# The routing-weight product of a two-block transformer kernel: contraction over 128 rows in place of a 32-row tile

## The chip, the core and the metric

The kernel runs on one core of a Trainium2 chip. The metric is device time in microseconds (us) from launch to end; the smaller the better. A core has five engines that work side by side and wait for each other through semaphores: TensorE (PE, with the weight loads shown apart as PEld), VectorE (DVE), ScalarE (ACT), GpSimd (POOL) and SyncE (SP), which starts the transfers here. TensorE multiplies a stationary operand, loaded first, with a moving operand that streams past it, and writes to one of eight PSUM banks; the other engines work in SBUF and read PSUM (POOL has no use of PSUM here).

## The reference

Two blocks run one after the other, each with attention and a feed-forward part, on 1024 tokens of width 256. Only the last part, a mixture of 16 experts of which each token uses 6, matters here:

```
logits = xf @ gate_w.T
probs = softmax(logits)
routing_weights, selected = top_k(probs, 6)
combine = zeros((T, 16)).at[arange(T)[:, None], selected].add(routing_weights)
act = silu(xf @ w1_gate.T) * (xf @ w1_up.T)          # 16 experts x 176 hidden columns
moe_out = einsum('te,tei,ehi->th', combine, act, w2)
out = x + moe_out + shared_out
```

`combine[t, e]` multiplies all 176 hidden columns of expert `e` for token `t`.

## The kernel before

**Numbers.** A product that must be exact to float32 is made of three fast products (`mm3`, L554): each operand is split into a high part, rounded to the type `float32r`, and the rest, and hi*hi, hi*lo and lo*hi are summed in PSUM.

**The last stage ("moe").** The hidden columns of the shared expert (3 chunks, j = 0 to 2) and of the 16 experts (22 chunks of 128, j = 3 to 24) stand one after the other; the tokens are in two halves of 512. A step (j, half) makes 12 products of 512 columns for gate and up. For j of 3 and more one product more follows on L690: it spreads the routing weights. Its stationary operand is a slice of 128 columns of `SELr`, a table of 32 rows that holds a one where a hidden column belongs to an expert (16 rows for the high part of the weights, 16 for the rest); its moving operand is 512 columns of `CTr`, the transposed routing weights of the half. The result is, for 128 hidden columns by 512 tokens, the weight that each must be multiplied with. There are 44 such products, 22 for each half. Then come 12 products of 256 columns (`down`) for the step before this one.

**Who feeds whom.** After a step ACT makes silu of the gate part (L1010), DVE multiplies it with the up part (L1357) and with the spread weights (L1364), ACT rounds it to its high part `VVh` (L1017), DVE subtracts to get the rest `VVl` (L1369), and TensorE's `down` takes both. One `down` is always a step behind, so that this chain has a whole step's time. PSUM banks 4 to 7 go round for gate, up and spread; banks 0 to 3 hold the sums.

**Order of the work.** A function `plan` writes one list of items, and each engine works through its own items in that order. Ahead of the moe steps stand `endnorm` (the last normalization; POOL's part is L1605), the splitting of the weight chunks moe3 and moe4 on POOL (L1654, L1656) and `selector` on POOL (L1694), which rounds `SELf`, as the transfer brought it, into `SELr`. `spread` turns the routing weights of a half on TensorE (L867) and ACT copies them into `CTr` (L1115). `latent_end()` names the events after which the memory of the attention stage may be overwritten.

Of the kernel before, what the change touches and what calls it, by code (L numbers as in the profile page):

```python
# [7 lines left out]
F32 = mybir.dt.float32  # L8
R32 = mybir.dt.float32r
BF16 = mybir.dt.bfloat16  # L10
I32 = mybir.dt.int32
ALU = mybir.AluOpType
# [3 lines left out]
T = 1024  # L16
# [35 lines left out]
class Signals:  # L52
# [10 lines left out]
    def mark(self, kind, *key, by=1):  # L63
        self.count[kind] = self.count.get(kind, 0) + by
        self.value[(kind,) + key] = self.sem(kind), self.count[kind]
        return self.sem(kind), by
# [4 lines left out]
    def at(self, kind, *key):  # L71
        return self.value.get((kind,) + key, (None, 0))
# [286 lines left out]
def build(nc, x, w, sm, sel, out):  # L359
    with ExitStack() as outer:  # L360
        S = Signals(lambda name: outer.enter_context(nc.semaphore(name)))
        B = Banks()
        program(nc, outer, S, B, x, w, sm, sel, out)


def program(nc, outer, S, B, x, w, sm, sel, out):
    mark, at, now = S.mark, S.at, S.now

    def sb(name, shape, dt=F32, ctx=outer):
        return ctx.enter_context(nc.sbuf_tensor(name, shape, dt))  # L370
# [89 lines left out]
    m1 = ExitStack()  # L460
# [1 line left out]
    U2 = [sb(f"U2{i}", [128, 512], ctx=m1) for i in range(3)]  # L462
    VV = [(sb(f"VVh{i}", [128, 512], R32, ctx=m1), sb(f"VVl{i}", [128, 512], R32, ctx=m1)) for i in range(3)]
    SELf = sb("SELf", [32, 22 * 128], ctx=m1)
    SELr = sb("SELr", [32, 22 * 128], R32, ctx=m1)
    CTr = sb("CTr", [32, T], R32, ctx=m1)
    parts += [(sb(f"yh{i}", [128, SLOT], R32, ctx=m1), sb(f"yl{i}", [128, SLOT], R32, ctx=m1)) for i in range(2)]
    m1.close()

# [8 lines left out]
    def bank(*key):  # L478
        return banks[B.of(*key)]
# [4 lines left out]
    def have(*key):  # L484
        return at(f"full{B.of(*key)}", *key)

    def vacates(*key):

        return S.sem(f"free{B.of(*key)}"), 1
# [10 lines left out]
    def half_cols(half):  # L500
        return slice(half * 512, half * 512 + 512)
# [35 lines left out]
    def latent_end():  # L537
        return have("lo", 3), at("hi", "u", n_units - 1), at("x3", 3), at("pn2", n_units - 1, 1)
# [364 lines left out]
    def scalar(x):  # L903
        e = Waits(x)
# [203 lines left out]
            x.activation(pr[:, hs, 0:16], pr[:, hs, 0:16], ACT.Exp).then_inc(*mark("ge", half))  # L1108

        def spread(half):  # L1110
            if half == 0:
                for s in latent_end():
                    e.wait_ge(*s)
            e.wait_ge(*have("sp", half))
            x.copy(CTr[:, half_cols(half)], bank("sp", half)[0:32, :]).then_inc(*vacates("sp", half))  # L1115

        run(order, {"norm1": norm1, "fuse": fuse, "turn1": turn1, "project": project, "headnorm": headnorm,
                    "turnqk": turnqk, "masks": masks_, "score": score, "pturn": pturn, "turnqm": turnqm, "turnat": turnat,
# [479 lines left out]
    def gpsimd(x):  # L1598
        e = Waits(x)
# [90 lines left out]
            rsqrt(rs, ve, half, "ve4", "rs4")  # L1690

        def selector():
            e.wait_ge(*at("sel"))
            x.tensor_scalar(SELr[:, :], SELf[:, :], 1.0, 0.0, ALU.mult, ALU.add).then_inc(*mark("selr"))  # L1694

        run(order, {"norm1": norm1, "rotate": rotate, "mask": mask, "l0begin": l0begin, "split": split, "memnorm": memnorm,
                    "memturn": memturn, "ffnmean": ffnmean, "expert": expert, "latstd": latstd, "l1norm": l1norm,
# [155 lines left out]
```

## Time and profile before

| what | value |
|---|---|
| median of 3 runs | 826.01 us (824.09 to 826.27) |
| the profiled execution | 827.4 us, of which 825.6 us are the span from the first to the last instruction |
| granted TensorE clock, mean | 0.946 of full speed |
| busy: PE / PEld / DVE / ACT / POOL | 741.5 / 599.1 / 473.3 / 322.4 / 245.0 us |
| chain of work that ended last, by engine | PE 71%, DVE 15%, ACT 5%, issue 5%, POOL 3% |
| the chain by line, first three | L554 48%, L649 4%, L620 4%; L690 2% |

All times in a trace count from the start of the span. A row of the timeline gives the start, the duration, the engine, the line and what is written and read; matmuls are pipelined, so that one starts before the one ahead of it has ended, and the distance from start to start, not the duration, says what one costs. "128\*128 128x512" is a tile of 128 rows by 128 columns of the array, and 512 columns of moving data; "32\*128 32x512" is a tile of 32 rows. The moe stage reaches from 567 us to the end.

### The profile page before, as it was taken

Reading aid. Unit: us, or ns where it says so; the run is one execution under the profiler, and the core shown is the slowest. Engines: PE = TensorE matmul, PEld = TensorE weight load, DVE = VectorE, ACT = ScalarE, POOL = GpSimd, SP = SyncE. Lnnn points to the kernel's source line nnn. Section 1 sums busy time; section 2 is a strip of 40 time slices with the busy share of each in tenths; the row PEclk is TensorE's granted clock in tenths of the full one; section 3 lists DMA queues with packets and bytes.
Section 4 is the critical chain, followed back from the end, with each engine's and each line's share of the span. In section 5 each row is a group of like instructions: output and inputs, shape, how many; then the busy total and the mean of one; then the engine's idle time right before and its main releaser. Section 6 shows DMA issues by size and latency. Waiting matters only on the chain.

```text
span 825.6 us, 11928 instructions
## 1 busy us (share of the span) xinstructions
PE 741.5 (90%) x4504; PEld 599.1 (73%) x4504; DVE 473.3 (57%) x1058; ACT 322.4 (39%) x771; POOL 245.0 (30%) x328
## 2 busy tenths in 40 slices
PE   4985599999886999797999998987999999999997
PEld 2764378788775888586778776765787777777775
DVE  4789768675448675656553545465344444454544
ACT  2423244544532333244664665572332222222221
POOL 1236411100325522407242333244132222233300
PEclk9988799999998899797998999899899999999999
DMA  6323000000202200001000000002011111111001
GB/s 208 96 65 96 11 1 2 1 2 1 64 20 57 58 2 21 20 20 39 1 1 1 2 2 1 2 1 58 18 39 44 52 39 39 39 39 39 1 1 52
DMA packets 11674, 25.84 MB, mean 31 GB/s; under 512 B 1344, under 2 KB 3392, under 8 KB 11584
## 3 DMA queue, kind: packets, MB, share of 16 engines
q1 hardware_dynamic: 11616, 25.07, 10.6%
q8 instruction: 36, 0.59, 0.3%
q14 instruction: 22, 0.18, 0.1%
HBM read 24.02 MB, written 1.05 MB: 30 GB/s over the span
## 4 chain that ended last, share of the span: by engine, by line
PE 71%; DVE 15%; ACT 5%; issue 5%; POOL 3%; DMA 1%; SPq 0%; DVEq 0%; POOLq 0%; ACTq 0%
PE ps L554 48%; PE ps L649 4%; PE ps L620 4%; PE ps L831 3%; PE ps L632 3%; PE ps L690 2%; ACT AO L1094 2%; PE ps L820 2%; PE ps L562 2%; DVE NB L1161 1%; PE ps L623 1%; PE ps L576 1%; DMA wr<-in_w 1%; PE ps L571 1%; PE ps L580 1%
## 5 line engine op out<-in xcount | busy, mean ns | idle before, releaser
L1685 POOL TENSOR_SCALAR PB<-PB,sml 128x256 f32<-128x256 f32 x128 | 59.2, 482 | 110.7 <-DVE sml L1519 110.7
L1357 DVE TENSOR_TENSOR U<-U,ps 128x512 f32<-128x512 f32 x50 | 34.4, 688 | 83.1 <-PE ps L554 83.1
L1017 ACT CAST VVh<-U 128x512 fp32r<-128x512 f32 x50 | 31.0, 621 | 123.4 <-DVE U L1364 109.0
L554 PE MATMUL ps<-ATh,wh 128*128 128x512 f32 x176 | 72.4, 411 | 4.7 <-POOL wl L1656 2.5
L554 PE MATMUL ps<-ATl,wh 128*128 128x512 f32 x176 | 71.1, 404 | 0.0
L554 PE MATMUL ps<-ATh,wl 128*128 128x512 f32 x176 | 70.9, 403 | 0.0
L1654 POOL TENSOR_SCALAR wh<-wr 128x768 fp32r<-128x768 f32 (+3 forms) x31 | 24.0, 773 | 148.7 <-PE ps L554 148.7
L1369 DVE TENSOR_TENSOR VVl<-U,VVh 128x512 fp32r<-128x512 f32 x50 | 45.7, 914 | 37.2 <-ACT VVh L1017 37.2
L1094 ACT COPY AO<-ps 128x512 f32<-128x512 f32 x64 | 34.8, 589 | 76.0 <-PE ps L820 76.0
L1082 ACT ACTIVATE PB<-ps,sml 128x256 f32<-128x256 f32 x128 | 59.6, 496 | 4.5 <-DVE sml L1513 4.5
L649 PEld LDWEIGHTS ps<-VK,PT 128*128 128x128 f32 x384 | 49.3, 191 | 12.0 <-issue 11.4
L1656 POOL TENSOR_TENSOR wl<-wr,wh 128x768 fp32r<-128x768 f32 (+3 forms) x31 | 55.9, 1805 | 2.6
L1010 ACT ACTIVATE U<-ps 128x512 f32<-128x512 f32 x50 | 29.9, 598 | 54.6 <-PE ps L554 54.6
L554 PE MATMUL ps<-wh,VVh 128*128 128x256 f32 x136 | 42.2, 311 | 8.0 <-DVE VVl L1369 8.0
L978 ACT ACTIVATE P<-SS 128x384 f32<-128x384 f32 (+1 forms) x48 | 26.8, 559 | 57.8 <-DVE SS L1312 57.8
L649 PE MATMUL ps<-VK,PT 128*128 128x33 f32 x384 | 46.8, 267 | 0.0
L1308 DVE TENSOR_REDUCE mx<-ps 128x2 f32<-128x384 f32 (+1 forms) x48 | 28.8, 600 | 26.3 <-PE ps L623 25.9
L1523 DVE TENSOR_TENSOR UTl<-ps,UTh 128x256 fp32r<-128x256 f32 x32 | 13.5, 423 | 52.7 <-ACT UTh L1100 52.7
L620 PE MATMUL ps<-KB,QKT 128*128 128x384 f32 (+1 forms) x96 | 43.4, 534 | 0.0
L554 PEld LDWEIGHTS ps<-ATh,wh 128*128 128x128 f32 x176 | 34.4, 195 | 12.4 <-POOL wl L1656 2.7
L820 PE MATMUL ps<-SM,PB 128*128 128x128 f32 x256 | 36.7, 289 | 6.4 <-DVE QHl L1137 4.5
L1502 DVE TENSOR_REDUCE sml<-ps 128x2 f32<-128x512 f32 x64 | 40.9, 681 | 2.0 <-PE ps L554 2.0
(255 smaller groups left out, 2153.7 us busy)
## 6 DMA issues: line engine op xcount, KB each, us to landing
wr<-in_w SPq DMA_DIRECT2D x32, 384.0 KB, 3.1
wr<-in_w SPq DMA_DIRECT2D x16, 321.0 KB, 3.0
wr<-in_w SPq DMA_DIRECT2D x11, 256.0 KB, 2.7
XO<-in_x SPq DMA_DIRECT2D x2, 512.0 KB, 4.7
out_dram<-XO SPq DMA_DIRECT2D x8, 128.0 KB, 1.8
wr<-in_w SPq DMA_DIRECT2D x2, 416.0 KB, 6.3
AO<-in_sm SPq DMA_DIRECT2D x1, 448.0 KB, 7.4
SELf<-in_sel SPq DMA_DIRECT2D x1, 352.0 KB, 4.2
```

The lines of the kernel that those rows point to most:

```text
L554: t = x.matmul(o, a, b, start=first and i == 0 and c == 0, stop=last and i == n - 1 and c == 2, skip_group_check=skip)
L620: x.matmul(bk[:, 0:n], QKT[:, g, b * 256 + qt * 128:b * 256 + qt * 128 + 128], KB[u % 2][:, h0:h0 + nh, cols], start=True, stop=False)
L649: p = x.matmul(o, pt[:, c * 128:(c + 1) * 128], vk4[:, t - qt + k, 8 * g + h, :], start=k == 0, stop=k == qt)
L820: p = x.transpose(bk[:, kc * 256 + qt * 128:kc * 256 + qt * 128 + 128], PB[i % 3][:, 2 * i2 + qt, kc * 128:kc * 128 + 128], ident)
L1017: x.copy((VV if run == "moe" else HH)[c][0][:, :], b[:, :]).then_inc(*mark("hi", "h", run, j, half))
L1082: a = x.activation(p[:, c, :], v[:, qt, :], ACT.Exp, bias=m[:, 8 + c:9 + c], scale=SC, accum_out=m[:, 12 + c:13 + c])
L1094: x.copy(PN[k % 4], bank("lt", i, i2)[:, :]).then_inc(*vacates("lt", i, i2))
L1357: x.tensor_tensor(b[:, :], a[:, :], bank("u", run, j, half)[:, :], ALU.mult).then_inc(*vacates("u", run, j, half))
L1369: x.tensor_tensor(hl[:, :], b[:, :], hh[:, :].bitcast(F32), ALU.subtract).then_inc(*mark("th", run, j, half))
L1502: x.tensor_reduce(m[:, 2 * i2:2 * i2 + 2], bank("ls", i, i2)[:, :].rearrange("p (q k) -> p q k", q=2), AX_X, ALU.max).then_inc(*mark("dv"))
L1656: x.tensor_tensor(lo[:, 0:k], raw[:, 0:k], hi[:, 0:k].bitcast(F32), ALU.subtract).then_inc(*mark("part", name))
L1685: t = x.tensor_scalar(p[:, c, :], p[:, c, :], m[:, 16 + c:17 + c], 1.0, ALU.mult, ALU.mult)
```

## The change

`SELr` and `CTr` get 128 rows in place of 32. The rows 32 to 127 of both are zero: POOL sets the whole of both tiles to zero in `selector` ahead of the copy of the 32 rows, and takes over the wait for `latent_end()` from ACT's `spread`, which waits for the zeros (`blank`) now. The product on L690 names the whole tiles and therefore contracts over 128 rows. Its text is not changed, and neither is its place, its bank or its number.

```
-    SELr = sb("SELr", [32, 22 * 128], R32, ctx=m1)
-    CTr = sb("CTr", [32, T], R32, ctx=m1)
+    SELr = sb("SELr", [128, 22 * 128], R32, ctx=m1)
+    CTr = sb("CTr", [128, T], R32, ctx=m1)
...
         def spread(half):
-            if half == 0:
-                for s in latent_end():
-                    e.wait_ge(*s)
+            e.wait_ge(*at("blank"))
             e.wait_ge(*have("sp", half))
-            x.copy(CTr[:, half_cols(half)], bank("sp", half)[0:32, :]).then_inc(*vacates("sp", half))
+            x.copy(CTr[0:32, half_cols(half)], bank("sp", half)[0:32, :]).then_inc(*vacates("sp", half))
...
         def selector():
+            for s in latent_end():
+                e.wait_ge(*s)
+            x.memset(CTr[:, :].bitcast(F32), 0.0).then_inc(*mark("blank"))
             e.wait_ge(*at("sel"))
-            x.tensor_scalar(SELr[:, :], SELf[:, :], 1.0, 0.0, ALU.mult, ALU.add).then_inc(*mark("selr"))
+            x.memset(SELr[:, :].bitcast(F32), 0.0).then_inc(*mark("selz"))
+            e.wait_ge(*at("selz"))
+            x.tensor_scalar(SELr[0:32, :], SELf[:, :], 1.0, 0.0, ALU.mult, ALU.add).then_inc(*mark("selr"))
```

On POOL, at the start of the moe stage, the kernel before has this order; `yh` and `yl` are the parts of the split chunks moe3 and moe4, `wr` a raw chunk, and in brackets stand the semaphores that an instruction waits for:

```order
L1605 TENSOR_TENSOR rs<-ve,negh 128x4 [waits s_ve4]
L1654 TENSOR_SCALAR yh<-wr 128x768 [waits s_x3,s_hi,s_pn2,s_full7,s_raw2]
L1656 TENSOR_TENSOR yl<-wr,yh 128x768 [waits s_part_hi]
L1654 TENSOR_SCALAR yh<-wr 128x768 [waits s_raw0]
L1656 TENSOR_TENSOR yl<-wr,yh 128x768 [waits s_part_hi]
L1694 TENSOR_SCALAR SELr<-SELf 32x2816 [waits s_sel]
L1654 TENSOR_SCALAR wh<-wr 128x768 [waits s_full4,s_raw1]
```

The same place in the changed kernel, whose lines are numbered two less up to here:

```order
L1654 TENSOR_TENSOR yl<-wr,yh 128x768 [waits s_part_hi]
L1693 MEMSET CTr 128x1024
L1695 MEMSET SELr 128x2816 [waits s_sel]
L1697 TENSOR_SCALAR SELr<-SELf 32x2816 [waits s_selz]
L1652 TENSOR_SCALAR wh<-wr 128x768 [waits s_full4,s_raw1]
```

Two MEMSETs stand ahead of the copy into `SELr` now. The first has no wait of its own left: the events of `latent_end()` were waited for by the split of moe3 five rows ahead. On TensorE, DVE, ACT and SP no instruction has been added, removed or moved.

## Rows read from the trace of the kernel before

**Rows 1.** Windows: busy us of PE, PEld, DVE, ACT, POOL; clock, DMA share, GB/s.
```profile
620.00:820.00 200.00, 199.03 (x1028) 155.26 (x1026) 96.12 (x128) 50.38 (x83) 50.78 (x34) 1.00 0.11 32
```

**Rows 2.** Chain that ended last, moe stage: start, us, engine and line.
```profile
642.49 0.42 PE ps L690
642.91 4.42 PE ps L554 x24
647.33 0.43 PE ps L690
...
812.14 0.43 PE ps L690
```

**Rows 3.** Timeline of PE around one spreading product.
```profile
700.26 0.39 PE L554 MATMUL ps<-ATh,wl 128*128 128x512 f32 x1
700.59 0.49 PE L690 MATMUL ps<-CTr,SELr 32*128 32x512 f32 x1
701.00 0.39 PE L554 MATMUL ps<-yh,VVh 128*128 128x256 f32 x1
701.23 0.28 PE L554 MATMUL ps<-yl,VVh 128*128 128x256 f32 x1
...
702.54 0.39 PE L554 MATMUL ps<-ATh,wh 128*128 128x512 f32 x1
...
705.11 0.39 PE L554 MATMUL ps<-ATh,wl 128*128 128x512 f32 x1
```

**Rows 4.** Timeline of the weight loads at the same place; in brackets idle time.
```profile
700.58 0.18 PEld L690 LDWEIGHTS ps<-CTr,SELr 32*128 32x128 f32 x1 [0.36 <-issue]
701.00 0.19 PEld L554 LDWEIGHTS ps<-yh,VVh 128*128 128x128 f32 x1 [0.24 <-issue]
```

**Rows 5.** Timeline of PE, feed-forward stage of block one, two `down` starts apart.
```profile
286.17 0.28 PE L554 MATMUL ps<-wh,HHh 128*128 128x256 f32 x1
...
294.61 0.28 PE L554 MATMUL ps<-xh,HHh 128*128 128x256 f32 x1
```

**Rows 6.** Timeline of PE, attention of block two, going over to 64 rows.
```profile
485.94 0.28 PE L554 MATMUL ps<-BTh,MTl 128*128 128x256 f32 x1
486.15 0.38 PE L554 MATMUL ps<-CDh,QHh 64*128 64x256 f32 x1
486.37 0.28 PE L554 MATMUL ps<-CDl,QHh 64*128 64x256 f32 x1
```

**Rows 7.** DVE's L1369: group of 620 to 820 us (min/median/max ns), then timeline.
```profile
L1369 DVE TENSOR_TENSOR VVl<-U,VVh x42: 692/693/1259, 620.4 to 819.3; 128x512 fp32r<-128x512 f32 x42
...
644.82 1.25 DVE L1369 TENSOR_TENSOR VVl<-U,VVh 128x512 fp32r<-128x512 f32 x1 [0.74 <-ACT VVh L1017]
...
578.22 1.65 DVE L1369 TENSOR_TENSOR VVl<-U,VVh 128x512 fp32r<-128x512 f32 x1 [0.68 <-ACT VVh L1017]
```

**Rows 8.** Timeline of DVE at the end of the last step.
```profile
817.09 0.69 DVE L1357 TENSOR_TENSOR U<-U,ps 128x512 f32<-128x512 f32 x1 [1.60 <-PE ps L554]
```

**Rows 9.** Timeline of POOL, from the copy into `SELr` to its next work.
```profile
576.76 2.57 POOL L1694 TENSOR_SCALAR SELr<-SELf 32x2816 fp32r<-32x2816 f32 x1
597.55 0.83 POOL L1654 TENSOR_SCALAR wh<-wr 128x768 fp32r<-128x768 f32 x1 [18.22 <-PE ps L554]
```

**Rows 10.** POOL's groups by line and shape: count, busy us, mean ns.
```profile
L1643 POOL MEMSET P<- 128x128 f32 x3 | 0.6, 205 | 0.8 <-PE ps L606 0.8
L1846 POOL MEMSET const-float32-0.0<- 128x1 f32 x1 | 0.1, 99 | 0.2 <-issue 0.2
```

**Rows 11.** Timeline of PE: first `down` of the moe stage, first spreading product.
```profile
579.93 0.58 PE L554 MATMUL ps<-wh,VVh 128*128 128x256 f32 x1 [6.95 <-DVE VVl L1369]
...
592.69 0.49 PE L690 MATMUL ps<-CTr,SELr 32*128 32x512 f32 x1
```

**Rows 12.** Windows, after two restarts of TensorE (at 270.72 and 579.93 us).
```profile
275.00:276.00 1.00, 1.00 (x9) 1.00 (x8) 0.00 (x0) 0.00 (x0) 0.92 (x2) 0.74 0.00 0
...
579.90:585.90 6.00, 5.97 (x22) 5.25 (x23) 1.26 (x2) 1.19 (x2) 0.00 (x0) 0.50 0.00 0
```

## The prediction

> **What bounds the kernel now.** I read the chain that ended last first, then the windows of the stage that the change touches, then TensorE's timeline inside one step. In the moe stage the chain is nothing but TensorE: a spreading product, 24 products of L554, a spreading product, and so on [rows 2]. The windows say the same: of the 200 us from 620 to 820 TensorE is busy 199.03, at full granted clock (1.00, the 2.4 GHz level), while DVE has 96, ACT 50 and POOL 51 us of work and DMA a share of 0.11 [rows 1]. So a nanosecond that a step loses or gains on TensorE is lost or gained at the end, until another engine comes into the way.
>
> From the spreading product at 642.49 to the one at 812.14 there are 35 rounds [rows 2]: (812.14 - 642.49) / 35 = 4.847 us a round. A round of the same 24 products without a spreading product stands in block one's feed-forward stage: the `down` at 286.17 and the one at 294.61 are two rounds apart [rows 5], 4.22 us each. So a spreading product costs 4.85 - 4.22 = 0.63 us, though it streams 512 columns as the products of gate and up do, and those stand 0.234 us apart (702.54 to 705.11, 11 steps [rows 3]).
>
> Where the excess lies shows in the starts [rows 3]. The product ahead of the spreading one starts 0.33 us before it, not 0.234; the first `down` product starts 0.41 us after it, not 0.234; and the second `down` product 0.23 us after the first, where the others need 0.119 (701.23 to 702.54, 11 steps). The weight loads say why: the load for the 32-row tile is put off by 0.36 us and the next load of a 128-row tile by 0.24, each starting together with its own matmul [rows 4], while elsewhere a load runs under the matmul ahead. The price is paid twice, once going in and once coming out. A change of the row count is what both have in common, and a second place bears it out: where the attention of block two goes over from 128 to 64 rows, the distances are 0.21 and 0.22 us where 0.119 is usual [rows 6].
>
> **The change part by part.** *The product.* With 128 rows, spreading products and their neighbours have one shape. By rows 3 the three distances become 0.234 + 0.234 + 0.119 = 0.587 us in place of 0.33 + 0.41 + 0.23 = 0.97: 0.383 us saved. By whole rounds it is 0.63 - 0.234 = 0.39. I take 0.385 a product. The product itself can't fall below 0.234, since it still streams 512 columns; the load of 128 rows takes 0.19 us beside 0.18 for 32 [rows 4], and fits under the 0.234 of the product ahead.
>
> How many of the 44 count? The last one does not: at the end DVE starts on the last gate and up parts at 817.09, released by L554 [rows 8], and the spread weights are wanted only after that, by when they are there. The other 43 lie on the path: 43 x 0.385 = 16.6 us.
>
> *Does the next engine hold?* The round becomes 4.847 - 0.385 = 4.46 us. DVE needs about 96.12 / 41 = 2.3 us of it, ACT and POOL 1.2 each [rows 1]. The chain from the end of the up part to `VVl` is the one to watch. In the round of 642.49 it is done at 644.82 + 1.25 = 646.07 [rows 7], 3.58 us after the spreading product began (a long case; the median of this line is 0.693 us). Its `down` starts two spreading products and a round's 24 products later: at 647.76 before, 5.27 us, and 0.234 + 4.46 = 4.70 after. So 1.1 us of slack are left, and this term costs nothing. The splits of the weights on POOL have more, with POOL idle three quarters of this stretch, and so have the transfers at a share of 0.11 [rows 1].
>
> *The two memsets on POOL.* The trace has memsets of one column at 0.099 and of 128 columns at 0.205 us [rows 10], so 0.83 ns a column: 0.95 us for `CTr` (1024) and 2.4 us for `SELr` (2816), together 3.4 us. The copy into `SELr` began at 576.76 and took 2.57 us [rows 9]; it would now end near 583.0 in place of 579.3. POOL's next work came at 597.55, after a wait for TensorE of 18.2 us [rows 9], and the first spreading product at 592.69 [rows 11]: more than 9 us of cover. `CTr` is blank near 577.7, and ACT copies into it what TensorE turns behind the first `down`, which starts at 579.93 [rows 11]: over 2 us of cover. The wait for `latent_end()` is met by then (the splits ahead of it wait for the same), and so is the one for the table's transfer, since the copy started without idle time behind the split. If that cover were gone, each microsecond late at 592.69 would be one at the end.
>
> *What the memsets do to DVE.* This is the one unknown. TensorE stood still for 6.95 us until 579.93, waiting for `VVl` of the first step [rows 11]. This DVE instruction began at 578.22 and took 1.65 us, not the usual 0.69 [rows 7]: it overlapped POOL's copy into `SELr`, which ended at 579.33, and finished 0.54 us after that. In the changed kernel the `SELr` memset stands at this moment (577.8 to 580.2). If a memset holds DVE back as the copy did, `VVl` ends near 580.8 and TensorE starts 0.9 us later; if it doesn't, `VVl` ends at 578.22 + 0.69 = 578.9 and TensorE starts 1.0 us earlier. No row of this trace has a POOL memset beside such a DVE instruction, so I take the middle, 0, and both ends for the range. The clock adds to it: after the idle stretch TensorE ran at 0.50 (the 1.2 GHz level) for 6 us, while after the restart at 270.72 it was back after some 5 us [rows 12]. A microsecond more or less at half speed is 0.5 us; I allow 0.7 either way.
>
> Here the Trainium skill has a rule (SBUF — State Buffer, section "Who interferes with whom"): a VectorE instruction with two SBUF inputs contends with a GpSimd instruction that reads SBUF, not with one that only writes it. The stretched `VVl` beside the reading copy agrees with its first half (1.65 against 0.69 us); its second half no row here shows. By it the memset lets `VVl` through, and the sum would be 1.0 us lower.
>
> *The sum.* 827.4 - 16.6 + 0 = 810.8 us for an execution like the profiled one, which stood 1.4 us above the median of the runs shown. Against the median, 826.0 - 16.6 = 809.4 us.
>
> **The rivals.** *Half the gain.* The loads stay uncovered on one side, for instance since the spreading product's own operands come from other engines than its neighbours'. Then about half is left, 43 x 0.19 = 8.3 us: 817.7. Against it: the products of gate, up and `down` change operands too, and lose nothing where the row count stays (4.22 us a round [rows 5]).
>
> *No gain.* The excess belongs to this product whatever its rows, and the change does not do what it says: 826.0, within what the memsets add or take (825 to 827). Against it speak the same excess at the change to 64 rows [rows 6] and its symmetry around the product [rows 3, 4]. The Trainium skill (TensorE: Matmul & The Clock Gate, the table "Why this matters for your kernels") says that a single matmul that contracts over 32 rows takes the same time as one over 128; taken by itself that rule gives this rival. The trace shows that what is at stake here is not the single matmul but its neighbours.
>
> *Slower.* POOL holds `VVl` through both memsets and the copy, until near 583.0 + 0.5: TensorE starts at 583.5 in place of 579.93, 3.6 us late. It decides only where the products give back less than 3.6 / 43 = 0.084 us each; with nothing from them the time is 826.0 + 3.6 = 829.6. It needs DVE shut out across two gaps between POOL's instructions, and the excess not due to the row count.
>
> **How the numbers follow.** The forecast, the whole gain, has 0.84; half the gain 0.08; no gain 0.05; slower 0.03. About 0.3% (2.5 us) is what a measurement of this kernel can tell from no change. The first two cases are faster by more than that: 0.92; no gain is within: 0.05; slower 0.03. The range: 0.36 to 0.40 us a product is 15.5 to 17.2 us; the start term is 1.0 and the clock 0.7 us either way; the runs before lay from 1.9 below their median to 0.3 above. Together 806.0 to 813.0, which holds nearly all of the forecast's 0.84. The predicted time is 809.4.
>
> **What would show it.** Right: the chain shows rounds of about 4.46 us; the spreading product stands 0.23 us from its neighbours and its weight load starts a product early; the stretch from 620 us on still has TensorE busy to the brim. The row of `VVl` near 578 us tells the memset's effect: 0.69 or some 2.5 us long. Wrong: rounds above 4.6 us, idle time of TensorE before `down` released by `VVl`, or a spreading product still 0.4 us from its neighbour at 128 rows.

## The result and the profile after

The changed kernel takes 813.04 us (median of 4 runs, 811.73 to 814.40), the kernel before 826.14 beside it; the ratio is 0.9844, with a 95% interval from 0.9819 to 0.987. So it is 13.1 us faster (10.7 to 15.0 by the interval), where 16.6 had been forecast: the time lies 0.04 us above the upper end of the range. The profiled execution took 811.7 us, with a span of 809.9.

The chain that ended last, in the moe stage (start, us, engine and line), answers to [rows 2]:

```profile
636.30 0.23 PE ps L690
636.53 4.22 PE ps L554 x24
640.75 0.23 PE ps L690
...
792.49 0.23 PE ps L690
```

From 640.75 to 792.49 there are 34 rounds: 4.463 us each, where 4.847 stood before and 4.46 was forecast. The timeline of PE around the first spreading product, and below it the weight loads at the same place, answer to [rows 3] and [rows 4]:

```profile
590.80 0.39 PE L554 MATMUL ps<-ATh,yl 128*128 128x512 f32 x1
591.03 0.39 PE L690 MATMUL ps<-CTr,SELr 128*128 128x512 f32 x1
591.26 0.28 PE L554 MATMUL ps<-wh,VVh 128*128 128x256 f32 x1
591.38 0.28 PE L554 MATMUL ps<-wl,VVh 128*128 128x256 f32 x1
```
```profile
590.80 0.19 PEld L690 LDWEIGHTS ps<-CTr,SELr 128*128 128x128 f32 x1
591.03 0.19 PEld L554 LDWEIGHTS ps<-wh,VVh 128*128 128x128 f32 x1
```

The three distances are 0.23, 0.23 and 0.12 us (0.33, 0.41 and 0.23 before), and each load starts a product ahead of its own matmul, without the idle time in brackets that it had. From 620 to 800 us TensorE has no idle time left:

```profile
620.00:800.00 180.00, 180.00 (x1008) 156.12 (x1008) 87.09 (x124) 48.91 (x81) 50.85 (x34) 1.00 0.12 35
```

(Window in us; then busy us of PE, PEld, DVE, ACT and POOL, granted clock, DMA share, GB/s; it answers to [rows 1].) So what is missing from the gain was lost before 620 us. It shows at the first `down` of the stage, the row that answers to [rows 11]:

```profile
579.88 0.58 PE L554 MATMUL ps<-wh,VVh 128*128 128x256 f32 x1 [10.29 <-DVE VVl L1367]
```

TensorE waits 10.29 us there, not 6.95. The timelines of DVE and of POOL tell why:

```profile
568.00 8.82 DVE L1159 TENSOR_SCALAR NB<-XO,mv,rs 128x256 f32<-128x256 f32 x4 [1.14 <-POOL rs L1603]
576.74 0.67 DVE L1355 TENSOR_TENSOR U<-U,ps 128x512 f32<-128x512 f32 x1
578.09 1.74 DVE L1367 TENSOR_TENSOR VVl<-U,VVh 128x512 fp32r<-128x512 f32 x1 [0.68 <-ACT VVh L1017]
```
```profile
571.60 1.80 POOL L1654 TENSOR_TENSOR yl<-wr,yh 128x768 fp32r<-128x768 f32 x1
573.34 0.95 POOL L1693 MEMSET CTr<- 128x1024 f32 x1
574.23 2.44 POOL L1695 MEMSET SELr<- 128x2816 f32 x1
576.76 2.53 POOL L1697 TENSOR_SCALAR SELr<-SELf 32x2816 fp32r<-32x2816 f32 x1
```

The four instructions that write the normalized half to `NB` stand right ahead of the first step's work on DVE. Before, they took

```profile
571.39 5.55 DVE L1161 TENSOR_SCALAR NB<-XO,mv,rs 128x256 f32<-128x256 f32 x4 [1.14 <-POOL rs L1605]
```

and the last ended at 576.94, just behind POOL's second split, when the copy into `SELr` ([rows 9]) began:

```profile
574.99 1.80 POOL L1656 TENSOR_TENSOR yl<-wr,yh 128x768 fp32r<-128x768 f32 x1
```

Now they take 8.82 us, 5.24 of it in the last of the four: it starts together with the second split, at 571.6, and ends at 576.82, only when both memsets are through. The memsets themselves took what had been worked out (0.95 and 2.44 us).

**A measure that leaves out the rest of the program.** Ahead of this place both kernels run the same instructions, yet POOL's part of the last normalization starts at 566.95 us in this profile and at 570.33 in that of before; over all profiles of this study it lies between 566.9 and 571.5. For comparing profiles I therefore count the stage from that row to the end of the span:

| kernel | start | span | stage | idle ahead of the first `down` |
|---|---|---|---|---|
| before | 570.33 | 825.6 | 255.3 | 6.95 |
| changed | 566.95 | 809.9 | 243.0 | 10.29 |

By this the change gave 12.3 us in the stage.

### The profile page after: what moved, and what is told of

Read it like the earlier page. It is cut to its first block, busy times and chain, and to the rows that moved or that the text cites. A ratio compares the mean times of both kernels' runs of the same rounds, so it can differ in the third digit from the quotient of the medians.

```text
span 809.9 us, 11931 instructions
## 1 busy us (share of the span) xinstructions
PE 722.9 (89%) x4504; PEld 601.7 (74%) x4504; DVE 470.2 (58%) x1058; ACT 321.8 (40%) x771; POOL 247.6 (31%) x330
## 4 chain that ended last, share of the span: by engine, by line
PE 71%; DVE 15%; issue 5%; ACT 5%; POOL 2%; DMA 1%; SPq 0%; DVEq 0%; POOLq 0%; ACTq 0%
PE ps L554 48%; PE ps L649 4%; PE ps L620 4%; PE ps L831 3%; PE ps L632 3%; ACT AO L1094 2%; PE ps L820 2%; PE ps L562 2%; DVE NB L1159 1%; PE ps L690 1%; PE ps L623 1%; PE ps L576 1%; DMA wr<-in_w 1%; DVE QKf L1261 1%; DVE T L1350 1%
## 5 line engine op out<-in xcount | busy, mean ns | idle before, releaser
L1367 DVE TENSOR_TENSOR VVl<-U,VVh 128x512 fp32r<-128x512 f32 x50 | 40.1, 802 | 37.2 <-ACT VVh L1017 37.2
L554 PE MATMUL ps<-wh,VVh 128*128 128x256 f32 x136 | 39.3, 289 | 11.7 <-DVE VVl L1367 11.7
```

Of the source, the lines that this page charges most:

```text
L554: t = x.matmul(o, a, b, start=first and i == 0 and c == 0, stop=last and i == n - 1 and c == 2, skip_group_check=skip)
L1367: x.tensor_tensor(hl[:, :], b[:, :], hh[:, :].bitcast(F32), ALU.subtract).then_inc(*mark("th", run, j, half))
```

## The experiments

Theory A: the product's term was right, and POOL's zeros cost what is missing, by holding the normalization on DVE. Theory B: the zeros cost nothing, and the gain was lost to the clock, or to waits that the shorter rounds bring. All experiments start from the changed kernel. The stage is counted as above.

| run | median us | ratio to before (95%) | stage | idle ahead of the first `down` |
|---|---|---|---|---|
| r1_after_again | 814.27 | 0.9848 (0.9815 to 0.9881) | 243.2 | 10.3 |
| r1_zeros_only | 830.67 | 1.0054 (1.0034 to 1.0075) | 259.6 | 10.29 |
| r1_zeros_late | 808.64 | 0.9786 (0.9753 to 0.982) | 237.7 | 5.98 |
| r1_gaps | 810.17 | 0.9797 (0.9764 to 0.983) | 237.9 | 5.99 |
| r2_rows64 | 831.38 | 1.0063 (1.0044 to 1.0082) | 259.9 | 10.30 |
| r2_gap_between | 810.33 | 0.9794 (0.9753 to 0.9836) | 239.8 | 6.87 |
| r2_reordered | 803.62 | 0.9732 (0.9705 to 0.9759) | 233.3 | 1.81 |

**The changed kernel again.** No edit.

> The changed kernel once more, for comparison with the runs beside it. If the missing part of the gain is lost at the start of the moe stage, by POOL's zeros holding the normalization on DVE, this run's first down waits about 10.3 us again (6.95 before) and the rounds of spreading product and 24 products take 4.46 us; time about 813. If the wait of 10.3 us was an accident of one execution, it is near 7 here.

Its idle time and its stage repeat to 0.2 us, while its span (814.6) is 4.7 us longer than the first profile's: nearly all of that arose before the moe stage. The wait is no accident.

**The zeros alone.** The tiles have 128 rows and are zeroed; the product keeps its 32.

```
-                x.matmul(b[:, :], SELr[:, (j - 3) * 128:(j - 2) * 128], CTr[:, sl], start=True, stop=True).then_inc(
+                x.matmul(b[:, :], SELr[0:32, (j - 3) * 128:(j - 2) * 128], CTr[0:32, sl], start=True, stop=True).then_inc(
```

> The tiles have 128 rows and POOL zeroes them as in the changed kernel, but the product names only their rows 0 to 31. Theory A (the zeros hold the last normalization instruction on DVE): rounds of 4.85 us as before, idle of TensorE ahead of the first down about 10.3 us, so slower than before by 2 to 3.5 us: 828 to 829.5. Theory B (the zeros cost nothing, the missing gain went into the clock or into waits that the shorter rounds bring): about 826, idle near 7 us.

Slower than before, as theory A has it, by somewhat more than it said. The chain has the old rounds, and PE the long wait:

```profile
643.08 0.42 PE ps L690
643.50 4.43 PE ps L554 x24
647.93 0.42 PE ps L690
```
```profile
584.39 0.58 PE L554 MATMUL ps<-wh,VVh 128*128 128x256 f32 x1 [10.29 <-DVE VVl L1367]
```

Its stage is 4.3 us longer than before's: the zeros, with the waits that go with them, cost that much, 3.3 us of it in this wait. And it is 259.6 - 243.1 = 16.5 us longer than the changed kernel's (mean of its two profiles): this is what the 128 rows are worth in the product alone, and 16.6 had been forecast for it. Theory B falls.

**The zeros later.** POOL waits until the first `VVl` is done.

```
             for s in latent_end():
                 e.wait_ge(*s)
+            e.wait_ge(*at("th", "moe", 0, 0))
             x.memset(CTr[:, :].bitcast(F32), 0.0).then_inc(*mark("blank"))
```

> The changed kernel with one wait more: POOL starts to zero only when the first VVl of the moe stage is done, so that nothing of DVE ahead of the first down can be held by it. Theory A: the normalization ends with POOL's second split, idle ahead of the first down about 6 us (VVl is no longer beside the copy either), time 3 to 4.5 us under the changed kernel: 808.5 to 810. Theory B: 813, with the first down no earlier or the gain lost again later.

As theory A has it. DVE and POOL:

```profile
568.06 5.57 DVE L1159 TENSOR_SCALAR NB<-XO,mv,rs 128x256 f32<-128x256 f32 x4 [1.14 <-POOL rs L1603]
...
574.90 0.69 DVE L1367 TENSOR_TENSOR VVl<-U,VVh 128x512 fp32r<-128x512 f32 x1 [0.69 <-ACT VVh L1017]
...
576.88 0.69 DVE L1367 TENSOR_TENSOR VVl<-U,VVh 128x512 fp32r<-128x512 f32 x1 [0.68 <-ACT VVh L1017]
```
```profile
575.66 0.95 POOL L1694 MEMSET CTr<- 128x1024 f32 x1 [2.18 <-DVE VVl L1367]
576.55 2.44 POOL L1696 MEMSET SELr<- 128x2816 f32 x1
```

The normalization takes 5.57 us, as before the change, and `VVl` has no POOL copy beside it: 0.69 us in place of 1.74. That is 4.3 us of idle time less than in the changed kernel; its stage is 5.4 us shorter, and the rest is TensorE's clock, of which more below. The second `VVl`, at 576.88, runs in the middle of the `SELr` memset and still takes 0.69 us: the memset doesn't hold this instruction.

**Gaps.** The zeros stay where they were, but POOL waits twice for its own work.

```
+            e.wait_ge(*at("part", "moe4"))
             x.memset(CTr[:, :].bitcast(F32), 0.0).then_inc(*mark("blank"))
+            e.wait_ge(*at("blank"))
             e.wait_ge(*at("sel"))
             x.memset(SELr[:, :].bitcast(F32), 0.0).then_inc(*mark("selz"))
```

> The changed kernel with two waits of POOL for its own work: the zeros of CTr wait until the split ahead of them has ended, those of SELr until CTr is zero. Both are met within some tens of ns, so POOL's work is the same. If DVE comes in wherever POOL has to wait for its own result, the last normalization instruction ends at the first of these gaps and the idle time ahead of the first down is 7 us; time near 809.5. If a memset holds DVE out as such, gaps or not, it stays at 10.3 us and 813.

```profile
571.79 5.55 DVE L1159 TENSOR_SCALAR NB<-XO,mv,rs 128x256 f32<-128x256 f32 x4 [1.14 <-POOL rs L1603]
...
578.62 0.69 DVE L1367 TENSOR_TENSOR VVl<-U,VVh 128x512 fp32r<-128x512 f32 x1 [0.68 <-ACT VVh L1017]
```
```profile
577.25 0.98 POOL L1694 MEMSET CTr<- 128x1024 f32 x1
578.29 2.45 POOL L1697 MEMSET SELr<- 128x2816 f32 x1
```

The same memsets at the same place, and the normalization is back to 5.55 us: it gets in at the first gap. So it is not the memset as such that keeps DVE out, but a memset that follows POOL's instruction ahead of it without a wait. And it takes a memset: in the changed kernel the first split ends at 570.68, POOL's next TENSOR_SCALAR follows it without a gap, and yet the second instruction of the normalization gets in between and ends at 570.83:

```profile
568.85 1.98 DVE L1159 TENSOR_SCALAR NB<-XO,mv,rs 128x256 f32<-128x256 f32 x1
570.65 0.86 POOL L1652 TENSOR_SCALAR yh<-wr 128x768 fp32r<-128x768 f32 x1
```

So did its last one in the kernel before, ahead of the copy into `SELr`. What sets the memset apart no run tells. `VVl` at 578.62 again runs beside the `SELr` memset unheld, which is why the idle time is 5.99 and not 6.95.

**A gap between the two memsets only.**

```
             x.memset(CTr[:, :].bitcast(F32), 0.0).then_inc(*mark("blank"))
+            e.wait_ge(*at("blank"))
             e.wait_ge(*at("sel"))
```

> The changed kernel with one wait of POOL for its own work, between the zeros of CTr (0.95 us) and those of SELr (2.44 us). If DVE's normalization gets in wherever POOL waits for its own result and nowhere else, it ends one memset of 0.95 us later than with a gap ahead of both, so the idle time ahead of the first down is 6.0 + 0.9 = 6.9 us, and the moe stage is about 1 us longer than with both gaps: time about 811. If only a gap at the end of the split counts, the idle time stays at 10.3 us and the time at 814.

```profile
571.89 6.44 DVE L1159 TENSOR_SCALAR NB<-XO,mv,rs 128x256 f32<-128x256 f32 x4 [1.14 <-POOL rs L1603]
```
```profile
577.23 0.95 POOL L1693 MEMSET CTr<- 128x1024 f32 x1
578.24 2.47 POOL L1696 MEMSET SELr<- 128x2816 f32 x1
```

The normalization is longer by the one memset, 6.44 - 5.55 = 0.89 us, and ends at 578.33, after the `CTr` memset and not after the `SELr` one. The idle time is 6.87 us, 6.9 had been expected. The stage is 1.9 us longer than with both gaps, not 1: the rest is TensorE's clock again.

**64 rows.** The product names the first 64 rows of both tiles.

```
-                x.matmul(b[:, :], SELr[:, (j - 3) * 128:(j - 2) * 128], CTr[:, sl], start=True, stop=True).then_inc(
+                x.matmul(b[:, :], SELr[0:64, (j - 3) * 128:(j - 2) * 128], CTr[0:64, sl], start=True, stop=True).then_inc(
```

> The changed kernel, zeros and all, but the product names the first 64 rows of both tiles. If what costs is any change of the row count between neighbours, a 64-row product pays as the 32-row one does: rounds of 4.85 us, weight loads that start with their own matmul, and a time like that of the zeros with the 32-row product, about 830. If the cost falls with the rows that lie idle, the round is between 4.46 and 4.85, near 4.7, and the time near 824.

```profile
699.67 0.40 PE L554 MATMUL ps<-ATh,yl 128*128 128x512 f32 x1
699.99 0.50 PE L690 MATMUL ps<-CTr,SELr 64*128 64x512 f32 x1
700.42 0.39 PE L554 MATMUL ps<-wh,VVh 128*128 128x256 f32 x1
700.64 0.28 PE L554 MATMUL ps<-wl,VVh 128*128 128x256 f32 x1
```
```profile
699.99 0.18 PEld L690 LDWEIGHTS ps<-CTr,SELr 64*128 64x128 f32 x1 [0.36 <-issue]
700.42 0.19 PEld L554 LDWEIGHTS ps<-wh,VVh 128*128 128x128 f32 x1 [0.24 <-issue]
```

The distances are 0.32, 0.43 and 0.22 us, the loads are put off by 0.36 and 0.24, and the stage is that of 32 rows (259.9 against 259.6), 16.8 us above the changed kernel's. This alone could also mean that any product of fewer than 128 rows is dear, whatever stands beside it. The kernel before tells otherwise, in the attention of block two, a few products behind [rows 6], where 64-row products follow each other:

```profile
486.96 0.27 PE L554 MATMUL ps<-CDh,QHh 64*128 64x256 f32 x1
487.07 0.28 PE L554 MATMUL ps<-CDl,QHh 64*128 64x256 f32 x1
487.19 0.28 PE L554 MATMUL ps<-CDh,QHl 64*128 64x256 f32 x1
```

They stand 0.11 and 0.12 us apart, as 128-row products of 256 columns do. What costs is the step from one row count to another, not how many rows are used.

**POOL's work in another order.** The zeros of `CTr` stand ahead of POOL's part of the normalization, and the splits and the rest of the selector wait for the first `VVl`.

```
+    item("zeros")
     item("endnorm", 1)
+    item("split", "moe3")
+    state["next"] += 1
+    item("selector")
     split(9)
-    item("selector")
...
                 for s in (attention_end() if PART[name] < 7 else latent_end()):
                     e.wait_ge(*s)
+                if PART[name] >= 7:
+                    e.wait_ge(*at("th", "moe", 0, 0))
...
-        def selector():
+        def zeros():
             for s in latent_end():
                 e.wait_ge(*s)
             x.memset(CTr[:, :].bitcast(F32), 0.0).then_inc(*mark("blank"))
+
+        def selector():
             e.wait_ge(*at("sel"))
```

> 128 rows, and POOL's work at the start of the moe stage put where DVE does not need SBUF: the zeros of CTr ahead of POOL's part of the last normalization, the splits of moe3 and moe4 and the rest of the selector only when the first VVl is done. The normalization should take 4 x 0.41 = 1.6 us in place of 8.8, and the idle time ahead of the first down fall from 10.3 to 2.5 us; then about 7 us less than the changed kernel, 806, unless moe3 or SELr come late for the steps that want them (then waits of TensorE for POOL, up to 3 us).

```profile
569.55 1.38 DVE L1162 TENSOR_SCALAR NB<-XO,mv,rs 128x256 f32<-128x256 f32 x4 [1.15 <-POOL rs L1606]
572.22 0.69 DVE L1370 TENSOR_TENSOR VVl<-U,VVh 128x512 fp32r<-128x512 f32 x1 [0.69 <-ACT VVh L1020]
```
```profile
572.97 0.39 PE L557 MATMUL ps<-wh,VVh 128*128 128x256 f32 x1 [1.81 <-DVE VVl L1370]
```

With nothing of POOL beside it the normalization takes 1.38 us in place of 8.82, and TensorE waits 1.81 us, less than the 2.5 expected. The zeros of `CTr` now lie ahead of the row from which the stage is counted, but they hide no time there, since POOL waits for DVE behind them:

```profile
568.50 1.02 POOL L1606 TENSOR_TENSOR rs<-ve,negh 128x4 f32<-128x4 f32 x1 [0.33 <-DVE ve L1157]
```

TensorE's first `down` product still runs at full clock (0.39 us, not 0.58); the clock falls only behind it, for some 3 us. The stage is 9.8 us shorter than the changed kernel's, and 803.62 us, 2.4 under what was expected, is the best time of this study. About half of this makes good what the zeros had cost; the other half is not the change's own, since POOL's splits held the normalization in the kernel before, too (5.55 us against 1.38).

## Why the prediction was right and where it was wrong

*The bound* was right: a round of TensorE is worth its length, and after the change TensorE is busy for 180.00 of 180 us.

*The product's term* was right in size and cause. Forecast: 43 x 0.385 = 16.6 us. Measured: 16.5 us between the kernel with the zeros and 32 rows and the one with 128, and 16.8 with 64 rows. The run with 64 rows, and the 64-row products that follow each other without the price, show that it belongs to the change of the row count. With that the rival of half the gain and that of no gain fall. The sentence of the Trainium skill that stood behind the latter (TensorE: Matmul & The Clock Gate, that a 32-row matmul takes the time of a 128-row one) doesn't settle it: the neighbours pay. Another page names what the loads show (TensorEngine Tiling (Array Packing), section "Key Properties": changing the tiling mode drains TensorE), and the trace agrees: 0.36 and 0.24 us of idle time of the loads, at 32 and at 64 rows, none at 128.

*The next engine* held from 620 to 800 us, with no wait; ahead of that one wait came that the prediction had put at nothing (0.73 us, below).

*The memsets' length and cover* were right: 0.95 and 2.44 us, and the copy behind them ended 11.7 us ahead of the first spreading product.

*What the memsets do to DVE* is the step that failed. It weighed one instruction, `VVl`, took 0, and allowed 1.0 us either way. The instruction that mattered was the one ahead of it on DVE, the last of the normalization. It stood behind POOL's second split already when the memsets began, and waited for both. I had read that `VVl` was stretched, 1.65 against 0.69 us, and had not looked at the row ahead: 5.55 us for four instructions that take 1.38 undisturbed, the last one ending with POOL's split. The measured size is +3.34 us of idle time in place of 0. The rival "slower" had the place (POOL holding DVE) and nearly the price (3.6 us), but hung it on `VVl` and on the case without a gain, so it never entered the range of the forecast, as a term of its own. It also took each change from one POOL instruction to the next for a gap at which DVE gets in; where a memset followed without a wait, DVE did not.

*The range*, too, doesn't add up as it is written: its parts, put together, reach from 826.0 - 17.2 - 1.0 - 0.7 - 1.9 = 805.2 to 826.0 - 15.5 + 1.0 + 0.7 + 0.3 = 812.5 us, not from 806.0 to 813.0.

*The rest of the sum*, from the windows of the two profiles, which tell how long TensorE ran at half clock (0.50):

```profile
579.90:581.90 2.00, 2.00 (x9) 2.00 (x10) 1.22 (x2) 0.62 (x1) 0.00 (x0) 0.50 0.00 0
581.90:583.90 2.00, 2.00 (x13) 1.76 (x12) 0.00 (x0) 0.51 (x1) 0.00 (x0) 0.78 0.00 0
595.90:597.90 2.00, 2.00 (x8) 1.51 (x7) 0.04 (x1) 1.89 (x3) 1.92 (x2) 0.63 0.00 0
597.90:599.90 2.00, 2.00 (x7) 1.62 (x6) 0.02 (x1) 0.24 (x1) 0.42 (x1) 0.52 0.24 45
```

These are of the changed kernel. Of before, [rows 12] show 6 us at 0.50 from 579.90 on, and the window behind them is

```profile
585.90:587.90 2.00, 2.00 (x11) 1.64 (x11) 0.13 (x1) 0.60 (x1) 0.00 (x0) 0.94 0.00 0
```

Behind its wait the changed kernel is back at full clock after 2.9 us, where the kernel before needed 6.2: (6.2 - 2.9) / 2 = 1.7 us gained. Then, behind 24 products of 16 columns (the gate of the second half, which every kernel here has), the clock falls once more, for 3.4 us: 1.7 us lost. This second fall stands in both profiles of the changed kernel and in those of the 64 rows and of the gap between the memsets, the four that were back at full clock after 2.9 us, and in no other. The allowance of 0.7 us for the clock was too small; that the two cancel is luck as far as the forecast goes, and why they come together is not shown. One wait more, 0.73 us, stands at 609.29, where POOL's next split came ahead of a `VVl`:

```profile
606.83 1.85 POOL L1654 TENSOR_TENSOR wl<-wr,wh 128x768 fp32r<-128x768 f32 x1
607.30 1.93 DVE L1367 TENSOR_TENSOR VVl<-U,VVh 128x512 fp32r<-128x512 f32 x1 [1.02 <-ACT VVh L1017]
609.29 0.38 PE L554 MATMUL ps<-yh,VVh 128*128 128x256 f32 x1 [0.73 <-DVE VVl L1367]
```

Every profile with the zeros has such a wait, also those at 32 and 64 rows. That of before has none: there `VVl` started 0.1 us ahead of the split, and the split was the longer one (2.30 us). In all profiles with the zeros ACT starts the rounding `VVh` of this step 0.37 us behind DVE's product, not 0.09 as before; at 32 and 64 rows that alone turns the order round, while at 128 rows the split also comes 0.3 us sooner behind the spreading product. Why ACT is late there is not shown. The section on the change says that nothing was added on ACT; the traces have one waiting instruction more there, ahead of the first copy into `CTr` (196 in place of 195 in all), and no run takes it away. Together: 16.6 - 3.3 + 1.7 - 1.7 - 0.7 = 12.6 us, and the stage measured 12.3.

## What to carry to other kernels

A product whose row count differs from its neighbours' is dear at both of its edges (0.39 us in all here): in a stream of TensorE that has no idle time, fill it up with zero rows. The filling itself is work for some engine: look at what stands in each queue beside the place where it goes, not only at the instruction that the end waits for, but at those ahead of it on the same engine. And when an instruction of DVE is stretched to several times its usual length in a trace, ask what POOL runs beside it before putting more on POOL there.

## What the runs showed of the hardware that I had not expected

A DVE TENSOR_SCALAR of 128x256 between two SBUF tiles was held by POOL's MEMSETs for as long as these followed POOL's work ahead of them without a wait: 3.3 us for two, 0.9 us for the one where a wait stood behind it, nothing where one stood ahead of it. A TENSOR_SCALAR of POOL that followed in the same way, without such a wait, let it in. The Trainium skill (SBUF — State Buffer, section "Who interferes with whom") says that a VectorE instruction in its 2-port mode and a GpSimd instruction exclude each other for the whole of an instruction. The trace agrees with the exclusion, if these instructions run in that mode, which no row tells; that the waiting side can lose its turn to two more instructions of the other the page does not say.

A TENSOR_TENSOR with two inputs in SBUF (`VVl`) ran beside the `SELr` MEMSET at its usual 0.69 us in three runs (r1_zeros_late, r1_gaps, r2_gap_between); beside POOL's copy, which reads SBUF, it took 1.65 us before and 1.74 in the changed kernel. That is the rule of the same section which the prediction drew on, and both halves of it are seen now. It didn't help the changed kernel, since `VVl` started 3.3 us later there and met the copy again.
